# An attention and feed-forward layer: another timetable for the jobs on shared PSUM banks, and the row-max products behind S^T

## The reference

```python
x = x + attention(layernorm(x), Wq, Wk, Wv, Wo, bo)     # x: (4, 1024, 128) f32, 16 heads of 64
x = x + ffn(layernorm(x), w_gate, w_up, w_down)         # hidden width 352
# attention: sim = q k^T * 64**-0.5 ; m = max(sim) ; e = exp(sim - m) ; e / (sum(e) + 1e-10) ; @ v ; @ Wo^T + bo
# ffn: every operand is quantised to FP4 and back, in blocks of 16 along the last axis (block maximum / 6 is
#      the scale), then h = silu(gate) * up ; down(h)
```

## Time and profile before

| | us |
|---|---|
| median of 3 runs | 1471.88 (1471.79 to 1472.68) |
| the profiled execution's own time | 1471.7 |
| its span, first to last instruction | 1469.9 |
| PE listed as busy | 1343.7 |
| mean granted clock of PE, share of full speed | 0.976 |

### The profile page before, as it was taken

One profiled execution on the slowest core, in us unless ns is written; L12 is line 12 of the kernel. 1 busy time (PEld: TensorE's weight loads), 2 busy tenths in 40 slices (PEclk: granted clock), 3 DMA queues, 4 the chain that ended last, 5 costly groups with the idle time before them and its releaser, 6 DMA issues.

```text
span 1469.9 us, 43046 instructions
## 1 busy us (share of the span) xinstructions
PE 1343.7 (91%) x17924; PEld 877.3 (60%) x17924; DVE 1109.4 (75%) x1717; ACT 1137.4 (77%) x2285; POOL 1138.6 (77%) x1135
## 2 busy tenths in 40 slices
PE   3899899989999999999999999999999999999955
PEld 2466565655666666666666666666666666666644
DVE  7677778667677878787787878778687877868577
ACT  2698787977887887888788787878878788787842
POOL 5688788878887877778788877878887787878832
PEclk8899999999999999999999999999999999999986
DMA  7111111111111112112111211211121111112000
GB/s 174 45 45 45 24 45 27 41 45 45 46 45 24 47 25 49 45 45 49 24 37 36 49 45 45 49 23 34 39 48 45 45 39 33 27 45 49 2 5 15
DMA packets 46688, 60.27 MB, mean 41 GB/s; under 512 B 8672, under 2 KB 21920, under 8 KB 46496
## 3 DMA queue, kind: packets, MB, share of 16 engines
q1 hardware_dynamic: 46336, 57.26, 16.7%
q10 hardware_dynamic: 160, 0.26, 0.0%
HBM read 4.80 MB, written 2.10 MB: 5 GB/s over the span
## 4 chain that ended last, share of the span: by engine, by line
PE 57%; DVE 26%; ACT 10%; issue 3%; POOL 2%; DMA 1%; SPq 0%; DVEq 0%; ACTq 0%
PE st L629 11%; DVE negm L960 10%; PE st L631 9%; PE sm L611 7%; PE ob L651 5%; ACT probs L782 5%; PE ob L658 5%; PE ob L656 4%; PE sm L565 3%; PE sm L549 2%; PE sm L560 2%; ACT o_n L792 2%; PE mb L549 2%; DVE v L926 2%; DVE q_small L1110 2%
## 5 line engine op out<-in xcount | busy, mean ns | idle before, releaser
L476 POOL TENSOR_TENSOR p_low<-probs 128x512 f16<-128x512 f32 x1024 | 1074.4, 1065 | 269.0 <-ACT probs L782 247.0
L782 ACT ACTIVATE probs<-st,lift,exp_scale 128x512 f32<-128x512 f32 x1024 | 768.5, 774 | 202.4 <-PE st L631 194.1
L960 DVE TENSOR_REDUCE negm<-sm 128x1 f32<-128x1024 f32 x512 | 615.3, 1213 | 218.1 <-PE sm L611 218.1
L629 PE MATMUL st<-q_hl,k_hh 128*128 128x512 f16 x1024 | 392.8, 384 | 13.8 <-ACT probs L782 12.5
L631 PE MATMUL st<-q_hm,k_l 128*128 128x512 f16 x1024 | 390.1, 381 | 0.0
L656 PEld LDWEIGHTS ob<-v,probs 128*128 128x128 bf16 x4096 | 290.7, 99 | 61.3 <-issue 0.8
L656 PE MATMUL ob<-v,probs 128*128 128x65 f16 x4096 | 320.4, 193 | 0.7 <-ACT o_raw L751 0.7
L658 PE MATMUL ob<-v,probs 128*128 128x64 f16 x4096 | 320.8, 194 | 0.0
L658 PEld LDWEIGHTS ob<-v,probs 128*128 128x128 bf16 x4096 | 271.7, 97 | 60.5 <-issue 0.8
L651 PEld LDWEIGHTS ob<-v,p_low 128*128 128x128 f16 x4096 | 177.8, 98 | 90.8 <-issue 1.3
L611 PE MATMUL sm<-k_hh,q_hl 64*128 64x512 f16 x512 | 156.4, 385 | 47.1 <-DVE k_low L915 21.1
(11 more groups left out here) (199 smaller groups left out, 1583.3 us busy)
## 6 DMA issues: line engine op xcount, KB each, us to landing
k_hh<-k_high SPq DMA_DIRECT2D x128, 128.0 KB, 2.4
k_l<-k_low SPq DMA_DIRECT2D x64, 128.0 KB, 2.4
q_hl<-q_high SPq DMA_DIRECT2D x64, 128.0 KB, 2.3
q_hl<-q_low SPq DMA_DIRECT2D x64, 128.0 KB, 2.4
q_hm<-q_high SPq DMA_DIRECT2D x62, 128.0 KB, 2.3
x<-x SPq DMA_DIRECT2D x4, 512.0 KB, 7.2
q_hm<-m_high SPq DMA_DIRECT2D x128, 1.0 KB
q_hm<-m_low SPq DMA_DIRECT2D x128, 1.0 KB
```

Of the source, the lines that this page charges most:

```text
L476: return pool.tensor_tensor(p_low[b][:, j, :], p, p.bitcast(BF16)[:, 1::2], ALU.subtract)
L629: pe.matmul(st[s % 2][:, :], k_hh[n][:, s * P:(s + 1) * P], q_hl[n][:, half * HALF:(half + 1) * HALF], start=True, stop=False)
L782: nc.scalar.activation(probs[k % 2][:, s, :], st[s % 2][:, :], ACT.Exp, bias=lift[:, 0:1], scale=exp_scale[:, head, pair:pair + 1]).then_i ...
L960: nc.vector.tensor_reduce(negm[k % 2][:, pair % 4:pair % 4 + 1], banks.rearrange("p a n -> p (a n)"), AX.X, ALU.max, negate=True).then_inc ...
```

## The change

`JOBS` and the `AT_...` constants get other places, and `scores` is called behind the S^T products of slots 0 and 4 instead of ahead of them. The turn of the maxima (m) goes from bank X1 at (k, 1) to bank MB at (k, 0), and DVE's part of it from (k, 2) to (k, 0). q0 and q1 change banks, q1 goes from unit 1 to unit 0 and t0 from unit 0 to unit 1; g0, u0, g1 and u1 leave slots 5 and 7 of units 1 and 2 for slots 1 and 2 of units 2 and 3; o0 goes from (1, 1) to (1, 5), o1 from (2, 1) to (2, 3), h0 from (1, 7) to (1, 6), h1 from (2, 3) to (2, 1), d from (2, 6) to (2, 5), w1 from (2, 7) to (3, 1), n1 from (3, 5) to (3, 1). In the preparation PE waits for the first maxima's rows in place of q's low part before it uses MB. In round 33 the late statistics come two and four slots later in DVE's order. No instruction is added or removed.

```diff
--- before.py
+++ after.py
@@ -48,26 +48,25 @@
 
 
 MB, X0, X1 = range(3)
-JOBS = [("m", X1, (0, 1), (0, 2), (0, 2)), ("k0", X0, (0, 1), (0, 2), (0, 2)), ("k1", MB, (0, 2), (0, 3), (0, 3)),
-        ("q0", X0, (0, 5), (0, 6), (0, 6)), ("t0", X1, (0, 6), (0, 7), None),
-        ("m", X1, (1, 1), (1, 2), (1, 2)), ("o0", X0, (1, 1), None, (1, 2)), ("q1", MB, (1, 2), (1, 3), (1, 3)),
-        ("t1", X0, (1, 5), (1, 6), None), ("x", MB, (1, 5), (1, 6), None),
-        ("g0", MB, (1, 7), (2, 0), (2, 2)), ("h0", MB, (1, 7), (2, 0), None), ("w2", MB, (1, 7), (2, 0), None),
-        ("m", X1, (2, 1), (2, 2), (2, 2)), ("o1", X0, (2, 1), None, (2, 2)),
-        ("h1", MB, (2, 3), (2, 4), None), ("w0", MB, (2, 3), (2, 4), None),
-        ("u0", X1, (2, 5), None, (2, 6)), ("n0", X0, (2, 5), (2, 6), (2, 6)),
-        ("g1", MB, (2, 7), (3, 0), (3, 2)), ("d", MB, (2, 6), None, (2, 7)), ("w1", MB, (2, 7), (3, 0), None),
-        ("m", X1, (3, 1), (3, 2), (3, 2)), ("u1", X0, (3, 1), None, (3, 2)), ("v0", MB, (3, 3), (3, 4), (3, 4)),
-        ("v1", X0, (3, 5), (3, 6), (3, 6)), ("n1", X1, (3, 5), (3, 6), (3, 6))]
+JOBS = [("m", MB, (0, 0), (0, 1), (0, 0)), ("k0", X0, (0, 1), (0, 2), (0, 2)), ("k1", MB, (0, 2), (0, 3), (0, 3)),
+        ("q0", MB, (0, 4), (0, 5), (0, 5)), ("q1", X0, (0, 5), (0, 6), (0, 6)),
+        ("m", MB, (1, 0), (1, 1), (1, 0)), ("t0", X1, (1, 1), (1, 2), None), ("x", MB, (1, 3), (1, 4), None),
+        ("o0", X0, (1, 5), None, (1, 6)), ("t1", X1, (1, 5), (1, 6), None), ("h0", MB, (1, 6), (1, 7), None),
+        ("m", MB, (2, 0), (2, 1), (2, 0)), ("g0", X0, (2, 1), (2, 2), (2, 2)), ("h1", X1, (2, 1), (2, 2), None),
+        ("w0", X1, (2, 1), (2, 2), None), ("w2", X1, (2, 1), (2, 2), None), ("u0", X1, (2, 2), None, (2, 3)),
+        ("o1", MB, (2, 3), None, (2, 4)), ("d", X0, (2, 5), None, (2, 6)), ("n0", X0, (2, 5), (2, 6), (2, 6)),
+        ("m", MB, (3, 0), (3, 1), (3, 0)), ("g1", X0, (3, 1), (3, 2), (3, 2)), ("w1", X1, (3, 1), (3, 2), None),
+        ("n1", X1, (3, 1), (3, 2), (3, 2)), ("u1", X1, (3, 2), None, (3, 3)), ("v0", MB, (3, 3), (3, 4), (3, 4)),
+        ("v1", X0, (3, 5), (3, 6), (3, 6))]
 ON_PE, ON_ACT, ON_DVE = 2, 3, 4
 
 
-AT_ROOT, AT_STATS, AT_NORM = (2, 0), (2, 0), (2, 3)
-AT_X, AT_X_END = ((2, 6), (3, 2), (3, 4), (3, 6)), ((0, 0), (1, 0))
-AT_H_BEGIN, AT_H = ((3, 6),), ((0, 0), (0, 4), (1, 0), (1, 4), (1, 6))
-AT_LN_STATS, AT_LN_MEAN, AT_LN = ((1, 0), (1, 4)), (1, 6), ((1, 2), (1, 4), (2, 0), (2, 2))
-
-AT_W = ((1, 0), (1, 0), (1, 4), (1, 6), (1, 6), (1, 6))
+AT_ROOT, AT_STATS, AT_NORM = (2, 3), (2, 2), (2, 5)
+AT_X, AT_X_END = ((2, 7), (3, 2), (3, 3), (3, 6)), ((0, 2), (0, 6))
+AT_H_BEGIN, AT_H = ((3, 6),), ((0, 2), (0, 3), (0, 6), (1, 2), (1, 3))
+AT_LN_STATS, AT_LN_MEAN, AT_LN = ((1, 2), (1, 6)), (1, 7), ((1, 2), (1, 4), (2, 0), (2, 2))
+
+AT_W = ((1, 2), (1, 2), (1, 4), (1, 6), (1, 6), (1, 6))
 AT_W2 = ((2, 2), (2, 2), (2, 4), (2, 6), (2, 6), (2, 6))
 W_QUANT = ((5, AT_W), (7, AT_W2), (8, AT_W))
 
@@ -516,7 +515,7 @@
                 turn_w(2, 1, st[1])
                 pe.wait_ge(s_ws[1], 1)
                 turn_w(1, 1, ob)
-                wait(pe, s_lo, 4)
+                pe.wait_ge(s_mr, 1)
                 turn_w(0, 1, mb[MB])
 
             def of_pair(w, m, g):
@@ -614,8 +613,6 @@
 
                     for s in range(SLOTS):
                         slot = 8 * k + s
-                        if has_max(r, k) and s % 4 == 0:
-                            scores(s // 4)
                         if cur:
 
                             n = 2 * q + head
@@ -631,6 +628,8 @@
                             pe.matmul(st[s % 2][:, :], k_l1[n][:, s * P:(s + 1) * P],
                                       q_hm[n][:, half * HALF:(half + 1) * HALF], start=False, stop=True
                                       ).then_inc(s_st, 1)
+                        if has_max(r, k) and s % 4 == 0:
+                            scores(s // 4)
                         if prev if k == 0 else cur:
 
                             pq, ph = (1 - q, 1) if k == 0 else (q, (k - 1) // 2)
@@ -978,10 +977,10 @@
                         ffn.beside_vector(dve, x2, r, (k, s))
                         if r == NPAIR + 1:
 
-                            if (k, s) == (1, 5):
+                            if (k, s) == (1, 7):
                                 dve.wait_ge(s_x2, 2 * NPAIR - 1)
                                 ffn.late_stats(dve, x2, 0)
-                            if (k, s) == (2, 3):
+                            if (k, s) == (2, 7):
                                 dve.wait_ge(s_x2, 2 * NPAIR)
                                 ffn.late_stats(dve, x2, 1)
```

## The result

The changed kernel takes **1487.68 us** (median of 5 runs, 1483.75 to 1490.54) against 1472.68 (5 runs, 1471.79 to 1482.71): ratio **1.0081, 95% interval [1.0041, 1.0121]**, slower by 0.8%. The forecast was 1438 and faster, with a range up to 1464. The profiled execution is one of the quick ones: 1483.75 us, span 1481.6. Against the span of before (1469.9) that is +11.7.

A forecast was written before the change was run, and what follows sets the result against it. TensorE bounds even rounds; odd rounds stand 3.8 us above it, waiting. 1471.7 - 27.5 (eleven pairs) - 8 (early rounds) - 0.5 (end) = 1435.7, plus 2.5 or so for thin covers: 1438 us; 1420 to 1464 at some eight in ten.

The forecast's parts named there:

- den at 0.15 us: Odd round, unit 0, VectorE: maxima, den and m_low done 3.75 us after S^T(0).
- rival B: VectorE's den kept out by POOL while it has several inputs ready, 6 us per odd round: 1502 us, chance 0.07.
- The hidden step at 2.3: Odd round, unit 0: hidden values' second step moves behind k_low(0), running from 4.4 to 6.7 us after S^T(0).
- q0's wait: Odd round, unit 0, slot 4: q0 uses bank MB and needs k1 taken; new PE wait of 0.8 us.
- o0 and v1: Odd round: new PE waits for the third maximum, 0.5 us at o0 in unit 1, 1.0 at v1 in unit 3.
- Rival A: VectorE becomes the bound of odd rounds, new waits double and pairs gain nothing: 1463 us, chance 0.10.
- S^T(0) is hidden: S^T(0) must wait for exp(6), ready after 1.5 us, but comes after 1.61: covered by 0.1 to 0.2 us.
- a turn behind 512 columns: Turning to half-array form behind a 512-column product was taken to cost the same as now; at most 26 us in all.
- odd round of 42.5: Odd rounds fall from 44.79 us by 2.3: 4.9 of waits go, 2.6 of new ones come.
- the 8 us up to round 10: Rounds 1 to 9 gain 8 us: 5 around the weights' steps, 1 in round 9, 2 from t1 elsewhere.
- Rounds 5, 7 and 8: Weights' steps hold PE up 12.7 us there; moved places leave 7.7 of waits, a gain of 5 us.
- the stall of 0.1: Slot 1: a job in a shared bank may start at 1.65 us, PE is there at 1.58; 0.1 us lost.

The follow-up runs named there:

- e9: The changed kernel with den (adding the small constant to four row sums) written as a reduction over one element, constant left out: 1429.89 us.
- e3: The changed kernel without den, the reciprocal taken of the row sums themselves: 1428.13 us.
- e8: The changed kernel with the row-max products ahead of S^T again, as before, and without den: 1428.49 us.
- e7: The changed kernel with den and the reciprocal ahead of the unit's first row maximum in VectorE's order: 1472.09 us.
- e2: The kernel before with the row-max products behind the S^T products, all places the old ones: 1491.96 us.
- e10: The changed kernel with each of GpSimd's p_low subtractions split into two halves, nothing left out: 1472.31 us.

## Why the prediction was wrong

- **The step that failed: den at 0.15 us.** "Counted from S^T(0): maxima, den and m_low to 3.75" took den at the median of the earlier trace rows. That row holds for the order of before, in which den fell into POOL's gaps or close to a seam. In e9, where den does take 0.15, the second maximum ends exactly there (529.38 to 533.13); in the changed kernel it ends at 4.5 (537.90 to 542.40), 0.75 late, all of it den's. The prediction itself had the needed sentence ("den now comes 0.35 us later against POOL's queue") and put it into rival B only; it did not let it touch the chain.
- **The hidden step at 2.3.** It took 2.8 (542.99 to 545.78), with L1109 and L1113 both caught near the start of a p_low, and 1.8 in e9, where L1109 starts ahead of POOL and L1113 near the end of a p_low. With den's 0.75 this is q0's wait: forecast 0.8, 1.9 with the 0.15 of modelled ends, and 0.2 to 0.4 when den is out (e3, e9). So without that contention the forecast would have been too high by 0.4.
- **o0 and v1.** Forecast 0.5 and 1.0, measured 1.3 and 1.5 as listed, and 0.3 to 0.4 each in e3 and e9. Together, 45.83 - 42.30 = 3.5 us of an odd round are the three waits' growth: 1.5 + 0.9 + 1.1.
- **The clock.** Not in the sum: in five odd rounds of eleven the products behind the wait at q0 ran at the lower clock, 4 x 1.36 + 1.20 = 6.6 us in the profiled execution and some ten in the median one, by the estimate above.
- **Rival B had the mechanism and the wrong size.** It was told as one den of 6 us an odd round, decided by POOL's having several inputs ready, 1502 us at 0.07. What came is 0.4 to 0.8 us in six of the eight units of a pair, by POOL's running instruction alone. The longest den of the changed kernel is 2.29 us, inside the bias instruction of 2.35 us that POOL began at 242.50; the one of 6.87 in round 4 is gone (2.09 at 170.01 now). Its own sentence against it, "once in 128", counted only waits that last through several instructions and overlooked the short ones.
- **Rival A** (VectorE becomes the bound) gave 1463 and is refuted by e9: with the same places and the same instructions, but for den's form, the three waits come to 1.0 us an odd round. The sign that was named for it, a wait at q0 above 1.5, did come (1.7), from den; the sign named for B, a den over 2 us in steady rounds, did not. So the signs as named pointed to the wrong rival.
- **Right:** every wait of the earlier trace rows went, the new ones stand where they were forecast, S^T(0) is hidden (PE waits 5.2 us for exps at S^T's first product in the whole kernel, 12.5 before), a turn behind 512 columns costs no more than the others (e8 against e3), and the odd round of 42.5 is what the change gives without den's wait (42.2 to 42.3). Even rounds were said to take 41.0 to 41.3 and take 41.57: the new order costs them 0.22 (e8 to e3, 41.34 to 41.56).
- **Right by luck: the 8 us up to round 10.** Measured were 9.3, but 6.9 of them are round 4 (46.97 us before, 40.05 after), where den took 6.87 us before and the prediction left that loss in its sum, and 2.2 came ahead of round 1. Rounds 5, 7 and 8, which were to give 5, gave 0.3 + 2.0 - 1.2 = 1.1, and round 9 lost 1.0 where it was to gain 1. In e9 those three give 4.5, so the estimate for them holds without den's wait. Round 4 is also most of why e9 lies 8 us below the forecast; its pairs gain 2.3 us each, against 2.5.
- **Two small slips in the sum.** The waits that stay in rounds 5, 7 and 8 add up to 2.0 + 1.7 + 0.9 + 2.8 = 7.4, not 7.7. And 0.43 + 1.14 is 1.57, not 1.65; the 1.65 fits only a maximum of 1.21, the length listed in the earlier trace rows, and the stall of 0.1 for k0, t0 and the others hangs on that difference. Neither changes the outcome.
- The 0.2% named as what a measurement can tell was too fine: the kernel before itself ran from 1470.6 to 1483.1 us in these runs.

## What to carry to other kernels

A short VectorE instruction that takes 0.15 us in the trace of before may be riding in another engine's gaps. Where a change shifts it, or the other engine, take the longest wait that engine's running instruction can make, here 1 us, into the chain, and count what stands behind it. Here it was cheaper to write it in a form that doesn't meet GpSimd at all (e9: one line, 58 us, without the constant, which changes no bit) than to look for a place for it (e7: a place that looked early was worse in even rounds).

## What the runs showed of the hardware that I had not expected

- A `tensor_scalar` of 128x4 float32 from SBUF to SBUF takes 0.15 us, or until just behind the next seam between GpSimd's instructions (0.90 to 0.93 us in three of the eight units of a pair with 1.04-us ones, 1.05 in one unit of e2's; with seams every 0.57 us the median is 0.34). A reduction or a reciprocal of the same 128x4 took 0.15 and 0.18 at any time.
- It can also miss seams: 8.60 us in e10, 6.87 in the earlier trace rows, 2.09 in the changed kernel (170.01 to 172.10, with POOL's run of ten p_low ending at 172.08): each time until POOL ran out. One in e10 missed a single seam, which came 0.04 us behind its start. Nothing here tells which den will miss.
- GpSimd is held up as well, by VectorE's product of 128x704 (L1113, L1114 in e2), and it matters which of the two begins first. In e2 the product began 0.12 us ahead of a p_low and took 0.89, while the p_low took 1.67 instead of 1.04. In the changed kernel it began 0.01 behind a p_low, which took its 1.04, and lasted 1.77; the p_low after that took 1.54. e2's VectorE and POOL, then POOL of the changed kernel:

```profile
553.33 0.89 DVE L1114 TENSOR_TENSOR qv<-hidden,q_small 128x704 f32<-128x704 f32 x1
```

```profile
553.46 1.67 POOL L476 TENSOR_TENSOR p_low<-probs 128x512 f16<-128x512 f32 x1 [0.66 <-ACT probs L782]
```

```profile
545.14 1.54 POOL L475 TENSOR_TENSOR p_low<-probs 128x512 f16<-128x512 f32 x1
```

- POOL busy for 40.3 of 42.6 us did not slow the steady rounds (e10); short instructions at a high share did less harm than long ones at 36 of 45.8.
